# Convolution with mixed weights: edge columns left out of the side taps' matmuls, and a new order of the work on every engine

## The reference

```python
N, Cin, H, W = (16, 256, 56, 56);  K, Cout, ks = (4, 256, 3)
pooled = jnp.mean(x, axis=(2, 3))
att = jax.nn.sigmoid(pooled @ att_w.T + att_b)
agg_w = jnp.einsum('nk,kocij->nocij', att, weight)
out = conv(x, agg_w, strides (1, 1), padding [(1, 1), (1, 1)])     # one sample at a time, its own weights
# layer: x = x + conv_ref(group_norm(x), ...), float32 in and out
```

## Time and profile before

| | us |
|---|---|
| median of 3 runs | 1393.18 |
| lowest and highest | 1392.3, 1393.21 |
| the profiled execution: its own time | 1391.56 |
| the profiled execution: first to last instruction (span) | 1390.0 |
| mean granted TensorE clock | 0.993 |

### The profile page before, as it was taken

One profiled execution on the slowest core, in us unless ns is written; L12 is line 12 of the kernel. 1 busy time (PEld: TensorE's weight loads), 2 busy tenths in 40 slices (PEclk: granted clock), 3 DMA queues, 4 the chain that ended last, 5 costly groups with the idle time before them and its releaser, 6 DMA issues.

```text
span 1390.0 us, 25354 instructions
## 1 busy us (share of the span) xinstructions
PE 1297.0 (93%) x8808; PEld 731.4 (53%) x8808; DVE 1190.4 (86%) x2006; ACT 925.6 (67%) x1466; POOL 57.3 (4%) x75
## 2 busy tenths in 40 slices
PE   0259999999999999999999999999999999999998
PEld 0125555555555555555555555555555555555554
DVE  3998898889988898988988899888989889898992
ACT  6656776676667677657776666777776577777531
POOL 0000000000000000000000000000000000000000
PEclk9979999999999999999999999999999999999999
DMA  9020555334455434445553344554344455534253
GB/s 366 2 93 1 140 140 140 90 104 112 120 137 141 125 93 118 109 117 140 140 132 82 104 112 132 141 141 119 91 120 111 120 140 140 139 79 129 51 135 120
DMA packets 29373, 165.70 MB, mean 119 GB/s; under 512 B 3360, under 2 KB 3616, under 8 KB 28192
## 3 DMA queue, kind: packets, MB, share of 16 engines
q1 hardware_dynamic: 20288, 113.94, 22.3%
q0 software_dynamic: 8928, 49.78, 21.2%
HBM read 112.33 MB, written 51.38 MB: 118 GB/s over the span
## 4 chain that ended last, share of the span: by engine, by line
PE 73%; DVE 14%; issue 10%; ACT 1%; DVEq 0%; POOL 0%; POOLq 0%; ACTq 0%
PE pM L428 67%; PE pG L403 6%; DVE Us L572 2%; DVE E L562 2%; DVE T L521 2%; DVE T L556 2%; DVE Vs L578 1%; DVE X L637 1%; DVE W L794 1%; DVE X L649 1%; DVE E L547 1%; DVE E L521 1%; DVE TB L630 0%; DVE TA L630 0%; PE pS L389 0%
## 5 line engine op out<-in xcount | busy, mean ns | idle before, releaser
L428 PE MATMUL pM<-Vs,Us 128*128 128x392 f16 x6912 | 1185.4, 332 | 27.2 <-DVE Us L572 14.0
L428 PEld LDWEIGHTS pM<-Vs,Us 128*128 128x128 f16 x6912 | 670.6, 98 | 530.9 <-issue 46.9
L839 ACT CAST Vs<-E 128x784 f16<-128x784 f32 x192 | 157.0, 844 | 167.0 <-DVE E L547 77.1
L521 DVE SCALAR_TENSOR_TENSOR T<-X 128x392 f32<-128x392 f32 x384 | 193.6, 558 | 7.7 <-ACT X L884 7.0
L578 DVE TENSOR_TENSOR Vs<-E,Vs 128x784 f16<-128x784 f32 x192 | 183.3, 970 | 0.7
L867 ACT ACTIVATE X<-pM,small 128x392 f32<-128x392 f32 x128 | 75.1, 587 | 117.7 <-PE pM L428 117.7
L849 ACT CAST Us<-E 128x768 f16<-128x768 f32 x128 | 102.9, 828 | 73.6 <-PE pM L428 41.5
L572 DVE SCALAR_TENSOR_TENSOR Us<-E,Us 128x768 f16<-128x768 f32 x128 | 119.1, 952 | 32.6 <-issue 30.3
L403 PE MATMUL pG<-W,D 128*32 128x512 f16 x1728 | 105.5, 390 | 31.3 <-DVE W L794 31.3
L905 ACT ACTIVATE unused<-X,small 128x784 bf16<-128x784 f32 x128 | 121.4, 949 | 6.3
L547 DVE SCALAR_TENSOR_TENSOR E<-T 128x784 f32<-128x784 f32 x128 | 119.1, 971 | 4.1
(11 more groups left out here) (75 smaller groups left out, 559.7 us busy)
## 6 DMA issues: line engine op xcount, KB each, us to landing
X<-x_dram SPq DMA_DIRECT2D x66, 784.0 KB, 5.5
out_dram<-X SPq DMA_DIRECT2D x64, 784.0 KB, 3.8
X<-x_dram POOLq DMA_DIRECT2D x62, 784.0 KB, 8.3
W<-w_dram SPq DMA_DIRECT2D x6, 1152.0 KB, 18.9
X<-w_dram SPq DMA_DIRECT2D x2, 1152.0 KB, 26.6
attw<-attw_dram SPq DMA_DIRECT2D x1, 128.0 KB, 8.5
small<-attb_dram SPq DMA_DIRECT2D x1, 0.5 KB, 10.2
```

The lines of the kernel that those rows point to most:

```text
L428: mm = pe.matmul(tile_rows(bank(k, o)), Us[:, j, a, c, o, kx, :], v_in(j, b, c, kx), start=(at < 2 and n == 0), stop=(n == 3 * KS * CT - 1 ...
L521: ins = dve.scalar_tensor_tensor(out=dst[c], in0=a[c], scalar=scale, in1=d[c], op0=ALU.mult, op1=ALU.add)
L839: act.copy(v_out(j, 0), e_planes(("V", *v))).then_inc(v_hi, 1)
```

## The change

Two things are done in one diff.

First, the planes in `Vs` lose their zero column: a plane is 392 contiguous elements (`U`), its rows 56 apart. A side tap no longer touches the edge: tap kx = 0 adds to output columns 1 to 55 from input columns 0 to 54, tap kx = 2 to output columns 0 to 54 from input columns 1 to 55, 7 runs of 55 each (`COLS`). [...] The writes of `v_high` and `v_low` become contiguous, and the zeros are no longer set at the start.

Second, the order in `epoch` is rewritten for TensorE, VectorE and ScalarE, and the tables with it. No instruction is added to a sample or taken from it; POOL and SP keep their order.

```diff
-VW = W + 1
-VROW = TR * VW + 3
+
+COLS = ((1, W), (0, W), (0, W - 1))
+KX = (1, 0, 2)
...
-        Vs = sb("Vs", [P, NC, 2, CT, VROW], F16)
+        Vs = sb("Vs", [P, NC, 2, CT, U], F16)
...
         def v_in(j, part, c, kx):
-            return Vs[:, j, part, c, kx:kx + TR * VW].rearrange("p (t w) -> p t w", w=VW)[:, :, 0:W]
+            first, last = COLS[kx]
+            return tile_rows(Vs[:, j, part, c, :])[:, :, first + kx - 1:last + kx - 1]
...
                 for c in range(CT):
-                    for kx in range(KS):
+                    for kx in KX:
+                        first, last = COLS[kx]
                         for a, b in ((0, 0), (0, 1), (1, 0)):
-                            mm = pe.matmul(tile_rows(bank(k, o)), Us[:, j, a, c, o, kx, :], v_in(j, b, c, kx),
-                                           start=(at < 2 and n == 0), stop=(n == 3 * KS * CT - 1),
-                                           skip_group_check=True)
+                            mm = pe.matmul(tile_rows(bank(k, o))[:, :, first:last], Us[:, j, a, c, o, kx, :],
+                                           v_in(j, b, c, kx), start=(at < 2 and n == 0),
+                                           stop=(n == 3 * KS * CT - 1), skip_group_check=True)
...
                 group(e, 5, 0)
+                if more:
+                    group_mean_mm(e)
                 group(e, 5, 1)
                 if more:
-                    group_mean_mm(e)
+                    group_var_mm(e)
                 group(e, 6, 0)
-                if more:
-                    group_var_mm(e)
                 group(e, 6, 1)
+                if more:
+                    logits_mm(e)
                 group(e, 7, 0)
-                if more:
-                    logits_mm(e)
                 group(e, 7, 1)
+                if more:
+                    mix(e, 0)
                 group(e, 8, 0)
-                if more:
-                    mix(e, 0)
                 group(e, 8, 1)
```

More of the change, by code:

```diff
@@ L312, in conv_kernel, with dve_count @@
         assert sorted(LAST) == sorted(DVE_TAKES)
-        assert LAST[:ND - 3 * CT] == DVE_TAKES[:ND - 3 * CT]
-        def last_count(takes):
-            return N * ND + max(LAST.index(t) for t in takes) + 1
+        def dve_count(e, takes):
+            order = LAST if isinstance(e, int) and e == N else DVE_TAKES
+            return e * ND + max(order.index(t) for t in takes) + 1
         block = ctx.enter_context(nc.Block())
@@ L676, in epoch @@
                 steps[0] = 0
-                u_low(e, (0, 1, 4))
-                v_pair(e, b, ("V", 0, 1, 1))
+                v_low(e, (0, 0, 5))
+                u_low(e, (0, 0, 0))
                 take_other(e, 2, 0)
+                v_low(e, (0, 0, 0))
+                take_other(e, 2, 1)
                 u_low(e, (0, 1, 0))
+                v_low(e, (0, 1, 1))
+                v_single(e, b, ("V", 0, 1, 5))
+                u_low(e, (0, 0, 5))
                 u_low(e, (0, 1, 5))
-                v_low(e, (0, 0, 0))
-                u_low(e, (0, 0, 5))
+                v_low(e, (0, 1, 2))
                 take_other(e, 3, 0)
-                take_other(e, 2, 1)
-                v_single(e, b, ("V", 0, 1, 5))
-                v_low(e, (0, 1, 2))
-                add_rows(e, b, 3, 0)
-                take_other(e, 3, 1)
-                v_low(e, (0, 1, 1))
-                v_low(e, (0, 0, 5))
-                take_edge(e, b, 4, 0)
                 v_pair(e, b, ("V", 0, 1, 3))
@@ L695, in epoch @@
                     channel_stats(e)
-                take_edge(e, b, 4, 1)
-                v_single(e, b, ("V", 0, 1, 0))
+                take_other(e, 3, 1)
+                take_edge(e, b, 4, 0)
                 if more:
                     group_shift(e)
-                take_edge(e, b, 5, 0)
+                take_edge(e, b, 4, 1)
+                add_rows(e, b, 3, 0)
                 v_low(e, (0, 1, 3))
@@ L703, in epoch @@
                     group_variance(e)
-                v_low(e, (0, 1, 4))
+                v_single(e, b, ("V", 0, 1, 0))
                 if more:
@@ L707, in epoch @@
                 v_low(e, (0, 1, 5))
+                take_edge(e, b, 5, 0)
+                v_low(e, (0, 1, 4))
                 take_edge(e, b, 5, 1)
+                if more:
+                    attention(e)
                 add_rows(e, b, 3, 1)
@@ L715, in epoch @@
                     v_low(e, (1, 0, 3))
+                    v_low(e, (1, 0, 2))
+                take_other(e, 8, 0)
+                if more:
                     v_low(e, (1, 0, 1))
+                    u_pair(e, ("U", 1, 0, 1))
+                take_other(e, 9, 0)
                 take_other(e, 8, 1)
                 if more:
-                    v_low(e, (1, 0, 2))
-                take_other(e, 8, 0)
-                take_other(e, 9, 0)
-                if more:
-                    u_pair(e, ("U", 1, 0, 1))
+                    add_rows(e, b, 9, 0)
+                    u_low(e, (1, 0, 1))
                     v_low(e, (1, 0, 4))
@@ L813, in _ @@
             u_low(0, (1, 1, 3))
-            u_low(0, (1, 0, 0))
-            v_single(0, 0, ("V", 1, 0, 0))
             u_low(0, (1, 1, 2))
             v_single(0, 0, ("V", 1, 0, 5))
+            v_single(0, 0, ("V", 1, 0, 0))
+            u_low(0, (1, 1, 4))
+            v_pair(0, 0, ("V", 1, 1, 1))
             first[0] = steps[0]
```

141 lines of the change are left out of this document (68 added, 73 removed), and 8 rows, old and new, of the table E_ITEMS.

## The result

The changed kernel takes 1368.33 us, the median of four runs (1366.15 to 1369.03), where the kernel before takes 1392.74 in the four runs of the same comparison (1390.88 to 1393.21). The ratio is 0.9825, with an interval from 0.9807 to 0.9842: 24.4 us less. The prediction was 1378, with a range from 1366 to 1392.

A forecast was written before the change was run, and what follows sets the result against it. TensorE's matmul stream was taken as the bound, VectorE close behind. Span 1390.0 - 19.6 (matmuls) + 3.9 (stops at jumps) + 0.9 (start) = 1375.2; with 1.6 twice to the median, 1378 us, range 1366 to 1392.

The forecast's parts named there:

- The bound: Whole kernel: TensorE's stream of matmuls sets the time, some 98.7% of a sample, with VectorE close behind.
- The columns: TensorE's group matmuls: shorter side taps and a one-run middle tap save 51 ns a group, 19.6 us over 384 groups.
- the price of a run: Group matmuls on TensorE: each run that starts anew costs about one column's time; seven runs make 2.7 ns a matmul.
- doesn't do what it says: Group matmuls: runs of 55 cost as 56, odd starts still paid; only the middle tap gains, 6 us; 1389, chance 0.07.
- The gap at VectorE's jump: VectorE's idle time at its loop jump: taken as 4.8 us, the middle between 3.6 and 6.0.
- The walk through VectorE's order: VectorE around its jump: branch at t = 14.9, next epoch at 19.7, `take_other` 3,1 seen by TensorE at 36.2.
- the wait of 3.2 us: TensorE behind each of six jumps, at t = 33.0: stands 3.2 us for VectorE; 19.2 us in all, 3.9 more than before.
- nothing for a run: Group matmuls: only columns count, groups save 32 us, loss at jumps grows 2 us; 1368, chance 0.13.
- The start: First group: waits on `u_low (1,1,1)`, which has one more `u_low` ahead; 0.9 us later taken, up to 1.5.
- `v_low` and `v_high`: VectorE's plane writes, now contiguous: given no gain, VectorE's load of 143.0 us a pair stays.
- Slower by its writes: Side taps' writes: 7 runs with holes cost extra columns; slower from 1.3 a hole, 1400 with 2; chance 0.09.
- The others fall behind in every sample: ScalarE's `sums` 1,1 await a late transfer, delaying `take_pair` 3,1, VectorE and TensorE: +14 us, 1392, chance 0.11.

The follow-up runs named there:

- z3: The changed kernel with the loop written out on all five engines, so no engine jumps back: 1358.76 us, ratio 0.9767.
- x3: The changed kernel with side-tap runs of 54 columns instead of 55, read from an even element and written from column 1: 1366.81 us in one execution.
- y5: The changed kernel with side-tap runs of 54 columns, both read and written from column 0: 1349.6 us in one execution.
- x1: The changed kernel's new order of every engine, with planes and taps as in the kernel before: 1383.6 us, ratio 0.9942.
- x2: The changed kernel's new planes and taps, in the order of the kernel before: 1377.99 us, ratio 0.9896.
- y4: The kernel before with POOL's transfer cut to the first 56 elements of each input block instead of 1568: 1382.76 us in one execution.
- x4: The changed kernel with a side tap writing its 385 columns as one contiguous run, reads unchanged: 1367.4 us in one execution.
- z1: The changed kernel unchanged, run again for a comparison on one chip: 1366.29 us, ratio 0.9817.
- z2: The changed kernel with ScalarE's `sums` 1,0 moved behind `take_pair` 3,0: 1366.03 us, ratio 0.9811.

## Why the prediction was right, and where it was off

**The bound.** Right. TensorE's stream sets the time, with and without the change: 78.86 of 78.90 us are busy in an undisturbed sample, and in z3 all of it.

**The columns.** Nearly the right sum (17.6 us for 19.6) from a wrong split. The step that failed is the price of a run. I took it as one column for each run that starts anew, so that runs of 55 would save their seven columns (2.9 ns) and keep paying for seven runs. In fact a run of 55 pays for 56, as x3 and y5 show beside each other: no column is saved at all. What the side taps gained, 2.5 and 1.7 ns, is that their rows lie 56 apart now and no run touches a 29th pair. The middle tap gained 3.3 ns and not 2.7, for the same reason. So (6 x 3.3 + 6 x 2.5 + 6 x 1.7) = 45 ns a group, where I had 51 and the groups show 46. That the sum came out near in spite of that is luck. That was the rival "doesn't do what it says" in its first half (pairs; a run of 55 costs what one of 56 costs), and I dismissed its second half the wrong way: I let odd starts be paid as before, though planes at an even distance end them for a run of 56, and for one of 55 they don't matter. With both halves right that rival's own reading would have given the measured saving.

**The gap at VectorE's jump.** This is the term that was mis-sized. I took 4.8 us, between 3.6 and 6.0, from the gaps of the old order, and said that the place moves and that the length isn't read off. It is 2.2 on the mean (1.6 to 2.6), outside my range, and what the runs showed in its place is this: the gap lasts until 1.4 to 1.8 us after a packet of kind "instruction" has landed, and that packet comes late where the DMA engines are full. x1 shows the short gap with the old taps (2.4 us at most), x2 the long one with the new taps in the old order (5.6), y4 one between, with less of the accumulating traffic. The trace of before had what was needed: its DMA engines are busy until t = 14.9 (599.3 less 584.4) and then idle, and the gap ends 1.5 us later. A branch at 14.9 would have met idle engines, and the gap could have been estimated at some 2 us, from the packet's own 0.3 and the 1.6 behind it. I read only its length, and took the new one from the old range.

**The walk through VectorE's order.** The branch comes at 589.84 (592.41 less 2.58), 13.7 us after TensorE's start of the sample at 576.13; I had 14.9. The difference is TensorE's own 1.05 us. The last group before the jump is done by TensorE's old clock, and I let it be done 3.0 us ahead of the late start. In samples without a jump the 14.9 stands (669.86 less 655.00). With 13.7 + 2.6 + 16.3 + 0.2 VectorE is done at 32.8, just ahead of the 33.0 at which TensorE asks. So the wait of 3.2 us didn't arise, and what is left of a jump is TensorE's own 0.8 to 1.2. The slip of the clock moves nothing in the sum: I had counted TensorE's own stop as part of the 3.2, so my loss of a jump is the gap less 1.6 (33.0 less 14.9, 16.3 and 0.2), and at least that stop, which is 3.2 with a gap of 4.8 and about 1 with 2.2. It is the gap that was wrong.

**The sum.** Of 19.2 us forecast as stops 5.7 came; with the late transfers 9.4, so 9.8 less. The columns gave 2.0 less than forecast, and the start took 0.6 more, against which the first sample gave 0.5 back. That makes the span 7.7 us shorter than the forecast one; measured it is 7.8 (1367.4 for 1375.2). The other 2 us of the distance between 1378 and 1368 lie in the step from the span to the median: I added 3.2, and it was 0.9.

**The range.** Its lower end, 1366, was said to be that of the rival "nothing for a run" with a short gap. By its own terms that case gives less: 1368 with the gap of 4.8, and 7 less, 1361, with 3.6. So too the forecast's own spread begins at 1371 and not at 1368. The measured 1368.33 lies inside the range as stated, but no case of the prediction has what happened, nearly the forecast saving with stops that shrink to 9.4 us; that the range holds the time is in part luck.

**The start.** 1.5 us later, the upper of the two values given (0.9 taken). **`v_low` and `v_high`.** Right at nothing: 970 ns before and after.

**The rivals.** "Nothing for a run" names the measured time almost to the microsecond (1368), and for the wrong reason: its 32 us of saving and 21 of stops (19.2 and the 2 more) were 17.6 and 9.4. It should not be taken as confirmed by the time. "Slower by its writes" falls with x4. "The others fall behind in every sample" was right in its mechanism, a late transfer ahead of `sums`, which holds up `take_pair`, VectorE and then TensorE; its size was off, a few stops of 0.2 to 1.3 us instead of 1 us in each sample, and z1 beside z2 can't tell its cost from nothing. The Trainium skill ("TensorE: Matmul & The Clock Gate", Back-to-back issue gap) gives N / 2.4 + 2.5 ns as the gap of an isolated matmul. In this trace it holds in a stream too for 392 columns in one run, 165.8 ns; it says nothing of runs.

## What to carry to other kernels

Lay out what a matmul reads and writes in runs that start at an even element and have an even length: by the reading above a run of 55 is as dear as one of 56 (165.8 ns for seven, as for 392 columns in one), and 56 from an odd start as dear as 58. Where a loop's jump back leaves an engine idle without a releaser, look at the DMA share in that gap before giving it a length: the same jump took 5 us under traffic and 2 without. The new order as a whole was worth 8.6 us, and writing the loop out another 7.5, where the new taps brought 14.2. When walking through an engine's order past another engine's own stop, keep the clock of the work that was done before that stop, or one sees a wait where there is none.

## What the runs showed that I had not expected

The length of the gap at a jump back, 1.6 to 2.6 us in the changed kernel where the DMA engines were nearly idle, 2.8 to 4.4 in y4 where stores and loads filled them, 3.6 to 6.0 in the kernel before with the accumulating transfers, and in each of them a packet of kind "instruction" that ends 1.4 to 1.8 us before VectorE goes on; TensorE's own jump cost 0.8 to 1.2 in the changed kernel. The program written out for all samples has no such gap and no stop, and fewer instruction packets than the loop has (108 against 163).

In these runs a matmul's time goes by pairs of elements within each run: 160.0 ns for 7 x 54 with even starts on both sides, 165.8 with the same reads and odd starts on the written side, the same as for 392 in one piece. Seven holes in the written columns cost nothing. Two values don't fit (166.7 for tap 2 in three kernels, and 168.3 for a tap that reads 385 in one run and writes seven of 55), and no run here settles them.
